# Tokenizer with one product for queries and keys in a new order; inverse deviations by logarithm and exponential

## Chip, cores and metric

The kernel runs on one core of a Trainium2 chip. The metric is the device time of one execution in microseconds (us), as the median of several runs. TensorE (PE) multiplies, with its weight loads (PEld) beside it; VectorE (DVE), ScalarE (ACT) and GpSimd (POOL) work on what it leaves in PSUM and in SBUF; SyncE (SP) issues most DMAs. Each engine takes its instructions strictly in the order in which they are written and is held up by semaphore waits only.

## What is computed

The input is 64 samples of 8192 values. A tokenizer makes 64 channels x 64 positions of each, and four residual layers follow, each on a layer-normed input:

```python
# tokenizer
h = maxpool(relu(bn(conv1d(h, w1, b1, 1, 1))), 8)
h = maxpool(relu(bn(conv1d(h, w2, b2, 1, 1))), 4)        # 64 channels x 128
q = Wq @ h + bq; k = Wk @ h + bk; v = Wv @ h + bv        # 8, 8 and 64 channels
h = gamma * (v @ softmax(q.T @ k).T) + h
h = bn(conv1d(h, w3, b3, 2, 1))                          # 64 x 64
# four layers
h = h + attention0(layernorm(h)) ; h = h + experts0(layernorm(h))     # attention0: norm, attention, norm, GELU MLP
h = h + attention1(layernorm(h)) ; h = h + experts1(layernorm(h))     # experts0 ends in a norm of its own
def _layernorm(x): return (x - m) / jnp.sqrt(v + 1e-5)
```

## The kernel before, in words

`PHASES` lists the stages: the tokenizer, a norm `n1` (in attention0 it is applied twice over, so it needs two inverse deviations, `twice=True`), attention0, `n2`, the GELU MLP, `n3`, experts0, `n5`, attention1, `n6`, experts1. Everything is FP32, and there is no planner: the order on each engine is the order in which the functions of a stage call each other.

**Tokenizer.** The 64 samples go through in eight groups of eight (`NG` = 8). For each group g: `conv1` (L251) makes four pieces h = 0 to 3, each into a pair of PSUM banks, and DVE's `reduce1` (L454) pools each piece; ACT's `relu1` (L557); `conv2` (L270) into banks 2 to 5, two `reduce2` (L470), ACT's `pooled` (L577); `keys_queries` (L296), one product for the keys into bank 2 and one for the queries into bank 3, which ACT copies out with its bias (L583, `t_k` and `t_q`); `values` (L306) and its copy (L589); `energy` (L315), DVE's `maxima` (L463), ACT's eight `exps` (L571), DVE's `soften` (L474 to L480), which normalises half of the probabilities while POOL's `half` (L226) does the other half; `turn` (L323) transposes them on PE and ACT's `turned` (L595) copies them out; `attend` (L332), DVE's `add` (L487) of the residual, `conv3` (L284), ACT's `last` (L561), which writes `h`, and DVE's `count` (L649), the statistics for the norm.

`steps` writes this as a `first()`, a `rest(g, b)` for g = 1, a loop of `rest` over g = 2 to 5, and four more calls of `rest` for g = 6 to 9 in which `among` leaves out what is not there. One `rest(g)` works on four groups at once: `turn(g-1)`, `keys_queries(g)`, `energy(g)`, `conv2(g+1)`, the pieces of `conv1` of groups g+1 and g+2, and `attend(g-2)` and `conv3(g-2)`. `weights(0..3)` (L346) are products of weights for attention1 that are done in gaps at the end, and `m.early[...]` are steps of attention0 that are called there.

**Loads.** SP issues the small constants and the first half of group 0, then (`load_rest`) all constants of the tokenizer in one DMA of 704 KB, group 1 of the input, then (`load_layers`) 3101, 1024 and 512 KB for the later stages, and only then, as PSUM and buffers allow, groups 2 to 7.

**Norms.** `norm` gives three parts: `variance` on DVE, `deviation` on ACT (`Sqrt` of variance + 1e-5, L690; for `n1` a second one, L692) and `inverse` on DVE (a `reciprocal`, L698; for `n1` also L701). Each norm is done for the first 48 samples and for the last 16 apart, and the calls stand inside the stages around it. experts0 has its own: `deviation` (L1801) and `normal` (L1671), once in each of its 16 groups of four samples, and in each group also one `Exp` for the gate (L1796). ACT needs a table for a function; where the next function is not in the one that is loaded, an `ACT_TABLE_LOAD` stands before it, written out (`preload_act_table`) or put in by the compiler.

## Time and profile before

| | us |
|---|---|
| median of 3 runs | 986.7 (983.88, 986.7, 989.49) |
| profiled execution | 982.16 |
| its span | 980.4 |
| tokenizer, to its last write of `h` | about 159 |
| experts0, the part in which all groups are alike | 340 to 570 |
| TensorE busy over the span | 924.4 (94%) |
| ScalarE busy over the span | 642.8 (66%) |

The profiled execution is one of its own, 4.5 us under the median of the three timed runs; the three lie 5.6 us apart. In the profile, a row of the timeline gives start, duration, engine, source line, operation, the tiles it writes and reads, their shapes and the number of merged instructions; the bracket at its end is the idle time of that engine just before, and what ended it. A table by stretches gives the busy time of each engine and the granted TensorE clock (1.0 is 2.4 GHz, 0.5 is 1.2 GHz, a value between is a mix of the two over the stretch).

### The profile page before, as it was taken

To read this page: it belongs to the slowest core of one execution; us is meant where nothing else is said; L and a number is where in the kernel's file an instruction comes from. 1 tells how busy PE (TensorE), PEld (TensorE's weight loads), DVE (VectorE), ACT (ScalarE), POOL (GpSimd) and SP (SyncE) were. 2 spreads that over 40 slices of the span, in tenths; PEclk is the share of its full clock that TensorE was granted. 3 is DMA by queue.
4 is the path that set the end of the run, shared out by engine and by line. 5 is a ranking of instruction groups with operands and counts; after the bars stand their busy time and mean duration, and the time that the engine had idled before them with its cause. 6 is when DMAs were issued, how large, how long until landed. Compare 5 with 4: busy or idle time off the path is not lost. (4 is left out here: it accounts for less than half of the span.)

```text
span 980.4 us, 35512 instructions
## 1 busy us (share of the span) xinstructions
PE 924.4 (94%) x12674; PEld 670.1 (68%) x12674; DVE 702.7 (72%) x1964; ACT 642.8 (66%) x1205; POOL 518.7 (53%) x814
## 2 busy tenths in 40 slices
PE   7899988999798999999999997899999999969998
PEld 2355556777566888888888884566666666658887
DVE  4577745777666577877878778788888888875553
ACT  1245556888666677877878775777777777754444
POOL 0001015888684578787887875455555656452110
PEclk8899998999999999999999998999999999999999
DMA  8624000000000000000000000000000000000001
GB/s 281 110 34 64 0 2 1 2 0 0 2 1 1 3 3 3 0 0 0 0 0 0 1 3 1 1 3 0 0 0 0 0 0 0 1 2 18 21 21 28
DMA packets 10961, 14.89 MB, mean 15 GB/s; under 512 B 9392, under 2 KB 9520, under 8 KB 9968
## 3 DMA queue, kind: packets, MB, share of 16 engines
q1 hardware_dynamic: 10704, 13.63, 6.1%
q8 instruction: 41, 0.67, 0.3%
q10 hardware_dynamic: 192, 0.39, 0.2%
q14 instruction: 24, 0.20, 0.1%
HBM read 11.92 MB, written 2.10 MB: 14 GB/s over the span
## 5 line engine op out<-in xcount | busy, mean ns | idle before, releaser
L1807 ACT ACTIVATE e_hid<-ps,cst 128x512 f32<-128x512 f32 x256 | 155.1, 687 | 53.7 <-PE ps L1579 53.7
L1514 POOL TENSOR_TENSOR e_acc<-e_acc,e_part 128x512 f32<-128x512 f32 x96 | 122.2, 1273 | 34.1 <-DVE e_part L1735 27.1
L1591 PEld LDWEIGHTS ps<-ew,e_hid 128*64 128x64 f32 x4096 | 124.8, 138 | 21.9 <-issue 10.4
L1591 PE MATMUL ps<-ew,e_hid 128*64 128x64 f32 x4096 | 133.8, 224 | 0.0
L1579 PE MATMUL ps<-e_xs,ew 64*128 64x256 f32 x1024 | 129.7, 393 | 0.0
L1735 DVE TENSOR_TENSOR e_part<-ps,e_wt 128x512 f32<-128x512 f32 x128 | 86.8, 687 | 44.5 <-PE ps L1591 39.6
L1579 PEld LDWEIGHTS ps<-e_xs,ew 64*128 64x128 f32 x1024 | 94.6, 189 | 15.7 <-issue 2.7
L2004 POOL TENSOR_TENSOR a_sum<-a_part 128x256 f32<-128x256 f32 x64 | 46.5, 727 | 94.0 <-DVE a_part L2112 93.9
L2073 PEld LDWEIGHTS ps<-cst,a_ex 128*128 128x128 f32 x512 | 56.6, 143 | 50.7 <-issue 50.7
L2101 DVE TENSOR_REDUCE a_rmax<-ps 128x8 f32<-128x1024 f32 x64 | 78.1, 1221 | 14.9 <-PE ps L2065 13.0
L226 POOL TENSOR_TENSOR t_prob<-t_ex,t_rscale 128x512 f32<-128x512 f32 x8 | 11.9, 1491 | 133.2 <-DVE t_rscale L477 133.2
L2104 DVE TENSOR_TENSOR a_diff<-ps,a_rmax 128x1024 f32<-128x1024 f32 x64 | 78.3, 1224 | 2.9
L2065 PE MATMUL ps<-a_u,a_xs 64*128 64x512 f32 x256 | 71.7, 637 | 8.3 <-DVE a_diff L2104 7.4
L2163 ACT ACTIVATE a_prob<-ps 128x1024 f32<-128x1024 f32 x64 | 65.5, 1023 | 17.7 <-PE ps L2073 17.2
L2089 PE MATMUL ps<-a_v,a_prob 128*64 128x66 f32 x2048 | 74.1, 224 | 0.6 <-DVE a_part L2112 0.6
L2073 PE MATMUL ps<-cst,a_ex 128*128 128x128 f32 x512 | 71.8, 283 | 1.6 <-ACT a_ex L2158 1.5
L2089 PEld LDWEIGHTS ps<-a_v,a_prob 128*64 128x64 f32 x2048 | 65.2, 137 | 11.4 <-issue 11.2
L2385 ACT ACTIVATE e_hid<-ps,cst 128x512 f32<-128x512 f32 x64 | 38.7, 687 | 50.4 <-PE ps L2261 50.4
L2158 ACT ACTIVATE a_ex<-a_diff 128x1024 f32<-128x1024 f32 x64 | 67.3, 1052 | 4.1 <-DVE a_diff L2104 3.5
L2146 ACT ACTIVATE a_u<-ps 128x1024 f32<-128x1024 f32 x32 | 32.8, 1025 | 34.6 <-PE ps L2041 34.6
L454 DVE TENSOR_REDUCE c_max<-ps 128x128 f32<-128x1024 f32 x32 | 38.9, 1222 | 15.7 <-PE ps L251 15.6
L2112 DVE TENSOR_TENSOR a_part<-ps,a_rec 128x512 f32<-128x512 f32 x64 | 44.3, 692 | 6.7
(258 smaller groups left out, 1994.0 us busy)
## 6 DMA issues: line engine op xcount, KB each, us to landing
x_in<-x_dram SPq DMA_DIRECT2D x42, 128.0 KB, 4.8
cst<-cst_dram SPq DMA_DIRECT2D x1, 3101.0 KB, 13.0
out_dram<-e_res SPq DMA_DIRECT2D x16, 128.0 KB, 2.0
ew<-ew_dram SPq DMA_DIRECT2D x1, 1024.0 KB, 15.1
cst<-cst_dram SPq DMA_DIRECT2D x1, 704.0 KB, 5.1
ew<-ew_dram SPq DMA_DIRECT2D x1, 512.0 KB, 16.9
x_in<-x_dram ACTq DMA_DIRECT2D x6, 64.0 KB, 3.7
x_in<-x_dram SPq DMA_DIRECT2D x6, 64.0 KB, 3.8
```

Source lines behind the costliest of these rows:

```text
L1514: eng.tensor_tensor(acc[:, :, :, :], acc[:, :, :, :], part[n % RING][:, :, :, :], ALU.add).then_inc(sum_sb.sem, 1)
L1579: mm = eng.matmul(m.ps[:, 4 - 2 * (n % 2) + r, j * 256:(j + 1) * 256], w1[rows, e * F0:(e + 1) * F0], T.xs[b][rows, :], start=True, stop=True)
L1591: mm = eng.matmul(m.ps[rows, 6 + n % 2, to:to + C], hid[e % 8][:, a:a + C], w2[:, e * C:e * C + C], start=True, stop=True)
L1735: eng.tensor_tensor(part[n % RING][:, :, :, :], m.ps[:, 6 + n % 2, :].rearrange("p (s j c) -> p s j c", s=TS, j=2), wt[b][:, :, 2 * n:2 * ...
L1807: nc.scalar.activation(hid[e % 8][:, :].rearrange("p (r t) -> p r t", r=2), m.ps[:, 4 - 2 * (n % 2):6 - 2 * (n % 2), j * 256:(j + 1) * 256 ...
L2065: mm = eng.matmul(m.ps[:, 2 + h, :], T.xs[b][rows, s * P:(s + 1) * P], u[b][rows, s, :, :].rearrange("p h t -> p (h t)"), start=True, stop ...
L2073: mm = eng.transpose(m.ps[:, 4 + j // 4, (j % 4) * P:(j % 4 + 1) * P], ex[s % 2][:, j, :], col(m, "ident"))
L2089: mm = eng.matmul(m.ps[rows, 6 + j // 4, (j % 4) * P:(j % 4) * P + W], prob[s % 2][:, j, rows], v[b][:, s, head * V:head * V + W], start=T ...
L2101: eng.tensor_reduce(rmax[:, :], src, AX, ALU.max).then_inc(max_sb.sem, 1)
L2104: eng.tensor_tensor(diff[:, :, :], src, bc(rmax[:, :], [P, H, P]), ALU.subtract).then_inc(diff_sb.sem, 1)
L2158: nc.scalar.activation(ex[s % 2][:, :, :], diff[:, :, :], ACT.Exp).then_inc(exp_sb.sem, 1)
L2163: nc.scalar.activation(prob[s % 2][:, :, :], m.ps[:, 4:6, :].rearrange("p a (j t) -> p (a j) t", t=P), ACT.Identity).then_inc(prob_sb.sem, 1)
```

## The change

It has four parts.

1. **One product.** The weights of keys and queries go into one matrix `wqk`, 64 columns for each of the two samples of a pair: columns 0 to 7 for the query and 32 to 39 for the key. `keys_queries` is one matmul into bank 2. ACT then makes two copies of 32 partitions for `k_sb` (which POOL has zeroed once, so that all other partitions are 0) and one of 128 partitions for `q_sb`: three activations in the place of two.
2. **A new order.** In a round, `attend` and `add` are of group g-1, not g-2, and stand just ahead of `energy(g)`; `values(g)` is in round g; `conv3(g-2)` follows the first `conv1` piece. On ACT `pooled` comes first and the exps are split 3 + 5, not 7 + 1. `first()` takes pieces 0 and 1 of group 1 ahead of `conv2(0)` (piece 1 into banks 6 and 7) with one matmul on zeros between them. The last rounds are written out as `tail()`, with `keys_queries(7)` and `values(7)` ahead of `turn(6)` and the four `weights` spread over it.
3. **Loads.** The weights of `conv2` have a DMA of their own ahead of group 1; the rest of the tokenizer's constants comes behind group 1.
4. **Inverse deviations.** `Sqrt` and `reciprocal` are replaced by `Ln` (of variance + eps), `Exp` with scale -0.5, and one Newton step on DVE of three small dependent instructions. `Ln` and `Exp` are in one table set (`LOGS`), which is loaded once at the start and again around the GELU MLP. `n1` has two of them and one more small DVE instruction.

The diff, cut to its core; the first `rest` is ScalarE's, the second VectorE's, and the last `deviation` is that of experts0.

```diff
-COLS += [("ident", P), ("w2", 3 * P), ("wq", P), ("wk", P), ("wv", P), ("w3", 4 * P)]
+COLS += [("w2", 3 * P)]
+TOK_B = sum(w for _, w in COLS)
+COLS += [("ident", P), ("wqk", P), ("wv", P), ("w3", 4 * P)]
...
-            for n, w in enumerate(("wk", "wq")):
-                eng.matmul(m.ps[:, 2 + n, :], col(m, w), x2[b][:, :], start=True, stop=True).then_inc(kq_ps.sem, 1)
+            eng.matmul(m.ps[:, kq_bank(g), :], col(m, "wqk"), x2[b][:, :], start=True, stop=True).then_inc(kq_ps.sem, 1)
...
         def rest(g, b):
+            pooled(g, b)
+            exps(g - 1, range(0, 3))
+            relu1(g + 1, 1 - b)
+            if known(g, 2):
+                last(g - 2)
+            exps(g - 1, range(3, GS))
+            turned(g - 1)
+            keys_queries(g)
+            values(g, b)
...
         def rest(g, b):
+            reduce1(g + 1, 1 - b, 3)
+            reduce1(g + 2, b, 0)
+            soften(g - 1)
+            reduce2(g + 1, 0)
+            reduce2(g + 1, 1)
+            reduce1(g + 2, b, 1)
+            if known(g, 2):
+                count(g - 2)
+            reduce1(g + 2, b, 2)
+            add(g - 1, 1 - b)
+            maxima(g)
...
         def keys_queries(g):
             eng.wait_ge(energy_ps.sem, energy_ps.at(g - 1))
+            eng.wait_ge(kq_ps.sem, kq_ps.at(g))
+            for rows in HALVES:
+                to, at = slice(rows.start, rows.start + 32), slice(rows.start + 32, rows.stop)
+                nc.scalar.activation(k_sb[to, :], m.ps[at, bank, :], ACT.Identity,
+                                     bias=col(m, "bk", at)).then_inc(kq_sb.sem, 1)
+            nc.scalar.activation(q_sb[:, :], m.ps[:, bank, :], ACT.Identity, bias=col(m, "bq")).then_inc(kq_sb.sem, 1)
...
-            nc.scalar.activation(dev[:, sl], var[:, sl], ACT.Sqrt, bias=m.eps[:, :]).then_inc(std_sb, 1)
+            nc.scalar.activation(log[:, sl], var[:, sl], ACT.Ln, bias=m.eps[:, :]).then_inc(log_sb, 1)
+            eng.wait_ge(log_sb, per * n + 1)
+            nc.scalar.activation(dev[:, sl], log[:, sl], ACT.Exp, scale=-0.5).then_inc(std_sb, 1)
...
+        def refine(eng, sl, first, v, shift, to, count):
+            eng.scalar_tensor_tensor(out=diff[:, sl], in0=first[:, sl], scalar=-0.5, in1=first[:, sl],
+                                     op0=ALU.mult, op1=ALU.mult).then_inc(root_sb, 1)
+            eng.wait_ge(root_sb, count + 1)
+            eng.scalar_tensor_tensor(out=m2[:, sl], in0=v[:, sl], scalar=shift, in1=diff[:, sl],
+                                     op0=ALU.add, op1=ALU.mult).then_inc(root_sb, 1)
+            eng.wait_ge(root_sb, count + 2)
+            eng.scalar_tensor_tensor(out=to[:, sl], in0=m2[:, sl], scalar=1.5, in1=first[:, sl],
+                                     op0=ALU.add, op1=ALU.mult).then_inc(ready, 1)
...
         def deviation(g):
-            nc.scalar.activation(y_dev[:, :], y_var[:, :], ACT.Sqrt, bias=m.eps[:, :]).then_inc(dev_sb.sem, 1)
+            nc.scalar.activation(y_log[:, :], y_var[:, :], ACT.Ln, bias=m.eps[:, :]).then_inc(log_sb.sem, 1)
+            eng.wait_ge(log_sb.sem, log_sb.at(g))
+            nc.scalar.activation(y_dev[:, :], y_log[:, :], ACT.Exp, scale=-0.5).then_inc(dev_sb.sem, 1)
```

**The start, on TensorE.** These are the first matmuls of before: four pieces of `conv1` of group 0 (L251, two matmuls each), `conv2(0)` (L270), three pieces of group 1, keys and queries (L296), the fourth piece, values (L306), piece 0 of group 2, energy (L315).

```order
L251 MATMUL ps<-x_in,w1s 128x512 x8
L270 MATMUL ps<-c,w2s 128x512 x12
L251 MATMUL ps<-x_in,w1s 128x512 x6
L296 MATMUL ps<-x,cst 128x512 x2
L251 MATMUL ps<-x_in,w1s 128x512 x2
L306 MATMUL ps<-cst,x 128x128 x4
L251 MATMUL ps<-x_in,w1s 128x512 x2
L315 MATMUL ps<-t_k,t_q 128x128 x8
```

And after, where the same steps are L268, L287, L312, L322 and L333, and L375 is the matmul on zeros:

```order
L268 MATMUL ps<-x_in,w1s 128x512 x10
L375 MATMUL ps<-warm 128x512
L268 MATMUL ps<-x_in,w1s 128x512 x2
L287 MATMUL ps<-c,w2s 128x512 x12
L268 MATMUL ps<-x_in,w1s 128x512 x4
L312 MATMUL ps<-x,cst 128x512
L322 MATMUL ps<-cst,x 128x128 x4
L268 MATMUL ps<-x_in,w1s 128x512 x2
L333 MATMUL ps<-t_k,t_q 128x128 x8
```

All of group 1's `conv1` now comes before keys and queries of group 0; piece 0 of group 2 still comes just ahead of the energy of group 0.

**A round of the loop, on TensorE,** from the transposes (before L323) to the energy. Before:

```order
L323 MATMUL ps<-cst,t_prob 128x128 x8
L246 ISA
L251 MATMUL ps<-x_in,w1s 128x512 x2
L292 ISA
L296 MATMUL ps<-x,cst 128x512 x2
L246 REGISTER_ALU
L251 MATMUL ps<-x_in,w1s 128x512 x2
L315 MATMUL ps<-t_k,t_q 128x128 x8
```

After (L341 transposes, L352 is `attend`):

```order
L341 MATMUL ps<-cst,t_prob 128x128 x8
L261 ISA
L268 MATMUL ps<-x_in,w1s 128x512 x2
L311 ISA
L312 MATMUL ps<-x,cst 128x512
L320 REGISTER_ALU
L322 MATMUL ps<-cst,x 128x128 x4
L261 REGISTER_ALU
L268 MATMUL ps<-x_in,w1s 128x512 x2
L352 MATMUL ps<-t_probT,v_tok 64x128 x8
L327 ISA
L333 MATMUL ps<-t_k,t_q 128x128 x8
```

Between the keys and queries and the energy that needs them stood one piece of `conv1`; now values, a piece of `conv1` and `attend` stand there. The first product's second matmul is gone.

**One group of experts0, on ScalarE,** from the gate's exponential to the norm's. Before:

```order
L1796 ACT_TABLE_LOAD
L1796 ACTIVATE e_gexp<-e_gap 128x4
L1805 REGISTER_ALU
L1807 ACTIVATE e_hid<-ps,cst 128x512 x2
L1805 REGISTER_ALU
L1807 ACTIVATE e_hid<-ps,cst 128x512 x2
L1799 ISA
L1800 REGISTER_ALU
L1801 ACT_TABLE_LOAD
L1801 ACTIVATE e_y_dev<-e_y_var,eps 128x4
```

After:

```order
L1860 ACTIVATE e_gexp<-e_gap 128x4
L1871 REGISTER_ALU
L1873 ACTIVATE e_hid<-ps,cst 128x512 x2
L1871 REGISTER_ALU
L1873 ACTIVATE e_hid<-ps,cst 128x512 x2
L1863 ISA
L1864 REGISTER_ALU
L1865 ACTIVATE e_y_log<-e_y_var,eps 128x4
L1867 ACTIVATE e_y_dev<-e_y_log 128x4
```

Both table loads of a group are gone, and one small activation is added. In the whole program 8 loads are left; they are at the start, around the GELU MLP and at the start of experts0.

## Rows read from the trace of the kernel before

**Rows 1.** Stretches of the span: length, busy time (instructions) per engine, clock.

```profile
0.00:31.25 31.25, 22.73 (x76) 8.86 (x76) 14.65 (x28) 7.32 (x11) 1.06 (x13) 0.89 0.91 266
61.42:124.33 62.91, 59.37 (x428) 33.09 (x429) 47.41 (x78) 31.55 (x95) 5.92 (x4) 1.00 0.22 32
124.33:158.20 33.87, 30.23 (x244) 22.17 (x244) 16.08 (x57) 18.66 (x53) 8.91 (x12) 0.95 0.01 1
340.00:570.00 230.00, 230.00 (x4401) 194.10 (x4403) 182.38 (x634) 175.38 (x295) 180.66 (x210) 1.00 0.00 1
```

**Rows 2.** Timeline of TensorE's matmuls in one round of the tokenizer's loop.

```profile
77.23 2.86 PE L270 MATMUL ps<-c,w2s 32*128 32x512 f32 x24 [0.33 <-ACT h L561]
...
81.65 1.13 PE L251 MATMUL ps<-x_in,w1s 48*128 48x512 f32 x4
82.71 1.98 PE L296 MATMUL ps<-x,cst 128*128 128x512 f32 x4
84.63 1.13 PE L251 MATMUL ps<-x_in,w1s 48*128 48x512 f32 x4
...
86.58 1.16 PE L306 MATMUL ps<-cst,x 128*128 128x128 f32 x8
87.67 1.09 PE L332 MATMUL ps<-t_probT,v_tok 128*64 128x128 f32 x16
...
93.00 2.86 PE L270 MATMUL ps<-c,w2s 32*128 32x512 f32 x24 [0.32 <-ACT h L561]
```

**Rows 3.** Timeline of the other engines in the same round.

```profile
84.73 0.69 ACT L583 ACTIVATE t_q<-ps,cst 128x512 f32<-128x512 f32 x1 [0.17 <-PE ps L296]
...
86.94 1.21 DVE L463 TENSOR_REDUCE t_nmax<-ps 128x8 f32<-128x1024 f32 x1
...
91.13 0.72 ACT L557 ACTIVATE c<-c_max,bi 128x512 f32<-128x512 f32 x1 [0.25 <-DVE c_max L454]
...
91.97 0.78 ACT L561 ACTIVATE h<-ps,bi,sc 128x512 f32 x1
```

**Rows 4.** Timeline of TensorE's matmuls in the first rounds.

```profile
14.28 5.50 PE L270 MATMUL ps<-c,w2s 32*128 32x512 f32 x24 [3.13 <-ACT c L557]
...
28.75 1.16 PE L306 MATMUL ps<-cst,x 128*128 128x128 f32 x8
31.26 1.13 PE L251 MATMUL ps<-x_in,w1s 48*128 48x512 f32 x4 [1.35 <-DMA x_in<-x_dram]
...
45.34 3.78 PE L270 MATMUL ps<-c,w2s 32*128 32x512 f32 x24
49.05 1.10 PE L323 MATMUL ps<-cst,t_prob 128*128 128x128 f32 x8
```

**Rows 5.** Timeline of the tokenizer's last rounds.

```profile
138.12 0.66 PE L323 MATMUL ps<-cst,t_prob 128*128 128x128 f32 x4 [1.47 <-DVE t_prob L480]
...
139.59 3.49 PE L296 MATMUL ps<-x,cst 128*128 128x512 f32 x4
...
158.32 0.78 ACT L561 ACTIVATE h<-ps,bi,sc 128x512 f32<-128x512 f32 x1 [1.24 <-PE ps L284]
```

**Rows 6.** Groups by line: table loads in experts0's loop (count, busy us, mean ns, idle before).

```profile
L1796 ACT ACT_TABLE_LOAD x13 | 16.7, 1283 | 0.2
L1801 ACT ACT_TABLE_LOAD x13 | 16.7, 1283 | 5.3 <-DVE e_y_var L1666 5.2
```

**Rows 7.** Timeline at four norms: n1, n3, n5 (late part), n6.

```profile
147.07 0.21 DVE L681 SCALAR_TENSOR_TENSOR norm_var<-norm_m,norm_dd 128x48 f32<-128x48 f32 x1
...
309.35 0.44 DVE L698 RECIPROCAL norm_rstd<-norm_dev 128x48 f32<-128x48 f32 x1
...
311.46 0.44 PE L793 MATMUL ps<-cst,e_xn 128*128 128x128 f32 x2 [3.14 <-POOL e_xn L781]
...
620.11 0.25 DVE L698 RECIPROCAL norm_rstd<-norm_dev 128x16 f32<-128x16 f32 x1 [2.69 <-ACT norm_dev L690]
...
865.61 1.07 PE L2073 MATMUL ps<-cst,a_ex 128*128 128x128 f32 x8 [1.26 <-ACT a_ex L2158]
```

More of the change, by code:

```diff
@@ L179, in steps, with known, pair, kq_bank @@
             rest(2 * i + 1, 1)
-        for g in range(NG - 2, NG + 2):
-            rest(g, g % 2)
-    def among(g, first=0, last=NG - 1):
-        return not isinstance(g, int) or first <= g <= last
+        tail()
+    def known(g, least):
+        return not isinstance(g, int) or g >= least
+    def pair(g, h):
+        return 0 if not isinstance(g, int) or g > 1 else 2 * h if g == 0 else 6 * (h % 2)
+    def kq_bank(g):
+        return 5 if isinstance(g, int) and g == NG - 1 else 2
     def load_half(eng, g, b, r, some=slice(0, H2), sem=None):
@@ L370, in rest @@
         def rest(g, b):
-            if among(g, 2, NG - 2):
-                values(g - 1, 1 - b)
-            last = not among(g, 0, NG)
-            tail = not among(g, 0, NG - 1) and not last
-            if last:
-                weights(3)
-            if among(g, 2, NG + 1):
-                attend(g - 2, b)
-            if among(g, 1, NG - 2):
-                conv1(g + 1, 1 - b, 3)
-            if tail:
-                weights(0)
-                m.early["a0_biases"](eng)
-            if last:
-                m.early["a0_turn"](eng)
@@ L411, in pe @@
         eng.wait_ge(prep, 1)
-        steps(eng, first, rest)
+        steps(eng, first, rest, tail)
     def dve(eng):
@@ L543, in dve @@
         m.left["tokenizer"] = last
-        steps(eng, first, rest)
+        steps(eng, first, rest, tail)
     def act(eng):
```

311 lines of the change are left out of this document (173 added, 138 removed).

## The prediction

> **What bounds the kernel now.** I read the table by stretches first [rows 1]: it tells which engine is full where. In the tokenizer's steady part, 61.42 to 124.33, TensorE is busy 59.37 of 62.91 us at full clock, DVE 47.41 and ACT 31.55; so TensorE is the bound there. In experts0, 340 to 570, TensorE is busy 230.00 of 230.00 us. At the two ends of the tokenizer it isn't full: up to 31.25 us it has 22.73 us of work at a mean clock of 0.89, in the last rounds 30.23 of 33.87 us at 0.95. The timelines of a round, of the start and of the end say what the gaps wait for [rows 2 to 5], and the groups by line what the table loads amount to [rows 6].
>
> **Part 1, one product less.** In a round the two products take from 82.71 to 84.63, 1.92 us [rows 2]; one takes half, 0.96. A round goes from the `conv2` at 77.23 to the one at 93.00, 15.77 us (62.91 over four rounds is 15.73), and holds about 0.3 us of waiting, for ACT's copy of `h`. If nothing else comes late, it becomes 14.8.
>
> **Part 2, is anything late in the new round?** I follow it from the start of `conv2` (time 0). Up to the next `conv1` piece, at 4.42 (81.65), nothing changes on PE: `conv2` and the transposes, which wait for soften. The five exps that now stand behind `h` on ACT take 5 x 0.34 = 1.7 us, soften some 0.6 to its scale, POOL's half 1.5: 3.85 with the 0.05 of starting late, where POOL ended at 3.8 before (81.01). So the transposes end where they did. Then: piece 4.42, product 5.48, values 6.44, piece 7.53, `attend` 8.55, energy 9.57, ending at 10.6. Energy needs three copies on ACT instead of two; each is 0.69 [rows 3], whatever its number of partitions I take it, since the row is for 512 elements a partition; 6.5 + 0.1 + 3 x 0.65 = 8.6, under 9.57: the third copy, 0.69 us, is hidden by values and `attend` (1.09 and 1.02, [rows 2]), with 1.0 to spare. Behind the energy PE has a piece, `conv3` and a piece: 1.02 + 1.93 + 1.03 = 4.0, to 14.6. On the other side DVE takes maxima 1.21 and a pooling of 1.23, then ACT `relu1` 0.72 and `h` 0.78 [rows 3]: 10.7 + 1.2 + 1.2 + 0.8 + 0.8 = 14.7, and `conv2` starts 0.25 later, at 14.95. The round is therefore 15.0, of which 0.35 is again a wait for `h`: **0.75 us less per round**, not the full 0.96. It holds for `conv2(2)` to `conv2(7)`, five rounds: 3.75 us. Bounds: 0 (something else is late by as much) and 5 x 0.96 = 4.8.
>
> **Part 3, the start.** The new order has group 1's `conv1` done early, since piece 0 needs no pooling of group 0 beyond the second. conv2(0) started at 14.28 after 3.13 us of idle and ran 5.50 us instead of 2.86, at the low level of the clock [rows 4]; now it starts at the same time (DVE's fold of the weights, `relu1`) but after pieces of group 1, so perhaps at full clock. Group 0's values then end near 22.6 instead of 29.9. It does not help: the next step, piece 0 of group 2, waits at 31.26 for its input [rows 4], and that DMA stands in SP's queue behind the same 4.6 MB for the later stages and only 64 KB less in front; I take the same 31.2. So TensorE stands idle for some 8.6 us, where it stood for 1.35. After 3.13 us of idle the clock was low for 5.5 us of work [rows 4]; I take it low until about 36. Then, with the durations of the low clock: piece to 33.2, energy 35.0, piece 36.6, conv2(1) 39.5 (37.6 before), two poolings and a third to 43.1, piece 3 of group 2 to 44.2, its pooling 45.5, conv2(2) 46.6 to 49.5 at the high clock, 51.8 at the low one. Before, it ended at 49.05 with 3.78 us for itself, partly low. I take **1.0 us later**; bounds: 2.7 later, and 0.6 earlier if the clock stays high throughout.
>
> The Trainium skill bears on this, on the page TensorE: Matmul & The Clock Gate (Part 1): a TensorE that has idled goes back to half clock, and is given full clock only after sustained work. By that rule the matmul on zeros protects conv2(0), where nothing is gained, and not the wait at 31 us. The trace agrees as far as it goes (5.50 us against 2.86 for the same `conv2`).
>
> **Part 4, the last rounds.** From conv2(7) at 124.33 to `h` of group 7 at 158.32 it is 34.0 us [rows 5]. There `turn(6)` waited 1.47 us for soften, and then the two products of group 7 ran at the low clock, 3.49 us. In `tail()` they are one product and stand ahead of `turn(6)`. Walking through as above from conv2(7) = 0: `turn(5)` to 4.5, a part of the weights 5.5, product 6.5, values, weights, `attend` 9.6, energy(6) 10.6; conv3(5) 12.6, product and values of group 7 to 14.7; DVE's maxima 11.9, ACT's eight exps 14.85, soften, POOL's half 17.0, `turn(6)` 17.7, `turned` 18.8, energy(7) 20.0, maxima 21.3, exps of group 7 to 24.4 (149.28 - 124.33 = 24.95 before). From there 0.85 us more goes, because before `turn(7)` stood behind eight weight products. Sum **1.4 us earlier**. Bounds: 0.5 later (the 1.5 us wait at 14.7 lowers the clock again) and 2.9 earlier (the 0.96 + 1.9 us that the second product cost in the two rounds, all of it on the path).
>
> **Part 5, the table loads.** Of 44 loads of 1283 ns, 36 go. 26 of them, 33.4 us of ACT time, are in experts0 [rows 6]. **They are hidden**: TensorE is busy for all 230 us of that stretch, and ACT for 175.38. Bounds: 0, and 33.4 if ACT were the bound. The new instructions there, one of ACT (0.3) and two of DVE (0.2 each) in a group of 17.25 us, are hidden in the same way: DVE has (230 - 182.38) = 47.6 us free, 3.6 in a group. What remains are the places where PE stands. Late part of n5: DVE waits 2.69 us for the deviation, whose load is in front of it [rows 7]; without the load it comes 0.93 earlier, the Newton step takes three times 0.25 (one such is 0.21, [rows 7]) where the reciprocal took 0.25: 0.3 gained. n6: PE waits 1.26 us for an exp that comes behind a load [rows 7]; DVE, with the longer Newton step in front of its next pooling, gives only 0.4. n2, n2's late part and n3 keep their loads of the GELU and get 0.3 to 0.4 us longer each, on the way to POOL, for whose result PE stands 3.14 us at n3 [rows 7]: 1.1 lost. n1 is even (ACT 0.8 earlier, DVE 1.3 later). n6's late part 0.1 lost. Together **0.5 us lost**; bounds 2.5 lost, 2 gained.
>
> The skill's page ScalarE: Activation LUTs (Rules for kernel authors) says to budget some 2.7 us for each switch of the table set; the rows have 1283 ns. By 2.7 us the two places that gain would gain about 2.8 us more in all, and the time would be 980.
>
> **The sum.** -3.75 + 1.0 - 1.4 + 0.5 = -3.65 us. The profiled execution of 982.16 becomes 978.5. It lies 4.5 us under the median of the three runs, 986.7; I keep that distance and forecast **983.0** for the median. What a measurement of this kernel can tell from no change is about 0.5%, 4.9 us, and the three runs of before are 5.6 us apart. So a gain of 3.65 us reads as the same.
>
> **Rivals.**
> A. *The start isn't lost.* If the clock recovers at once after the wait for group 2 and stays high in the last rounds, the start gives 0.6, the end 2.9: 3.75 + 0.6 + 2.9 - 0.5 = 6.75 us, 979.9. For it: in before, after 1.35 us of idle there, the clock stayed high. Against it: the idle is six times as long now.
> B. *The new round chains through `add` and `pooled`: slower.* On ACT `pooled(g+1)` now stands ahead of the exps of group g, and it waits for `add(g-1)`, which waits for `attend`, at 9.6: 10.7 to 11.4 in my count, and the exps can start at 12.0. The slack is 0.65 us. From the point where `add` is later than that, each round passes from PE to DVE, ACT and back, `relu1` and `h` behind the exps, and PE stands. At 1.0 us more than before per round it is +5.0, with +1.0 -1.4 + 0.5: 5.1 us slower, 991.8. Against it: DVE's pooling before `add` ends at 9.9, and POOL is out of it.
> C. *The loads did cost.* The weight loads of PE wait here and there for `e_hid`; if a third of the 33.4 us were on the path, 11 more us go, 972. Against it the 230.00 of 230.00.
> D. *No gain.* The start loses its 2.7, the end nothing gained and 0.5 lost on norms: 0.55 us earlier, 986.2.
>
> **Chances.** Forecast 0.49, A 0.28, D 0.11, B 0.08, C 0.04. Faster by over 0.5%: A, C, and 0.06 of the forecast's own spread, 0.38. Slower: B, 0.08. Within: 0.54. The range goes from A less the 2.8 us that half the spread of the three runs makes, 977, to D plus as much, 989; it leaves out C and B.
>
> **What would show it.** The steady round: `conv2` to `conv2` near 15.0 us. One product of 1.0 us. Piece 0 of group 2 again near 31.2 with an idle of 8 to 9 us before it, and 2 us long. conv2(2) ending at 49.5 to 52. `h` of group 7 near 32.6 us behind conv2(7). experts0's group again 17.25 us, with ACT some 30 us less busy. I am wrong if group 2 lands well before 31 us, if the round is over 15.5, or if experts0 gets shorter.

## The result and the profile after

| | before | after |
|---|---|---|
| median of 7 runs each, us | 985.3 (983.5 to 989.5) | 989.7 (988.2 to 993.0) |
| ratio, 95% interval | | 1.0042 [1.0024, 1.0061] |
| profiled execution, us | 982.16 | 988.21 |
| span, us; mean granted clock | 980.4; 0.977 | 986.5; 0.965 |
| busy PE, DVE, ACT, us | 924.4, 702.7, 642.8 | 928.5, 741.0, 606.7 |

The changed kernel is 4 us slower, and the interval excludes a ratio of 1; 983.0 with 977 to 989 was forecast. The first view is again the table by stretches: length, busy time of PE, PEld, DVE, ACT and POOL, granted clock, DMA. Its four rows answer to [rows 1].

```profile
0.00:31.98 31.98, 24.88 (x76) 9.45 (x76) 14.53 (x28) 7.18 (x12) 1.53 (x14) 0.84 0.95 258
63.55:121.90 58.35, 55.53 (x428) 32.54 (x429) 44.41 (x76) 34.14 (x99) 5.93 (x4) 1.00 0.23 34
121.90:157.16 35.26, 30.75 (x233) 23.92 (x234) 18.65 (x62) 19.77 (x64) 8.31 (x12) 0.85 0.01 1
340.00:570.00 230.00, 229.60 (x4392) 193.22 (x4390) 211.20 (x644) 143.24 (x280) 179.90 (x210) 1.00 0.00 1
```

The steady part is 58.35 us where it was 62.91. The last rounds, from `conv2(7)` to `h` of group 7, are 35.26 us where they were 34.0, and at a mean clock of 0.85 where it was 0.95. In experts0 no table load of [rows 6] is left and ACT is 32 us less busy, as forecast; DVE is 29 us busier, which was not.

The timeline of TensorE in a round, which answers to [rows 2]:

```profile
78.30 2.86 PE L287 MATMUL ps<-c,w2s 32*128 32x512 f32 x24 [0.65 <-ACT h L587]
...
83.46 1.12 PE L312 MATMUL ps<-x,cst 128*128 128x512 f32 x2
84.42 1.05 PE L322 MATMUL ps<-cst,x 128*128 128x128 f32 x8
...
87.49 1.16 PE L333 MATMUL ps<-t_k,t_q 64*128 64x128 f32 x16
...
92.72 0.71 PE L287 MATMUL ps<-c,w2s 32*128 32x512 f32 x4 [0.49 <-ACT h L587]
```

One product of 0.96 us (83.46 to 84.42) and a round of 14.42; over four rounds 58.35 / 4 = 14.59, against 15.73. The third copy is hidden, the energy waits for nothing, and 0.5 us of waiting for `h` is left.

The first rounds, which answer to [rows 4]:

```profile
14.13 2.08 PE L268 MATMUL ps<-x_in,w1s 48*128 48x512 f32 x4 [2.60 <-DMA x_in<-x_dram]
...
20.15 4.81 PE L287 MATMUL ps<-c,w2s 32*128 32x512 f32 x24
...
31.98 1.13 PE L268 MATMUL ps<-x_in,w1s 48*128 48x512 f32 x4 [1.70 <-DMA x_in<-x_dram]
...
41.96 2.08 PE L268 MATMUL ps<-x_in,w1s 48*128 48x512 f32 x4 [2.55 <-DVE c_max L478]
...
47.47 4.81 PE L287 MATMUL ps<-c,w2s 32*128 32x512 f32 x24
52.21 1.09 PE L341 MATMUL ps<-cst,t_prob 128*128 128x128 f32 x8
```

TensorE now waits for group 1's input too (until 14.13), and `conv2(0)` runs at 20.15, where it ran at 14.28. `turn(0)` is at 52.21, 3.2 us later than in [rows 4]. The wait of 2.55 us at 41.96 is one of the new order. It was 1.42 at the same place before (the first two lines are DVE's in after, the third is TensorE's in before):

```profile
38.42 2.36 DVE L494 TENSOR_REDUCE c_max<-ps 128x256 f32<-128x1024 f32 x2 [1.58 <-PE ps L287]
40.69 1.21 DVE L478 TENSOR_REDUCE c_max<-ps 128x128 f32<-128x1024 f32 x1
40.11 1.81 PE L251 MATMUL ps<-x_in,w1s 48*128 48x512 f32 x4 [1.42 <-DVE c_max L454]
```

DVE now does both `reduce2` of `conv2(1)` ahead of the `reduce1` for which the next piece of `conv1` waits. Before, it did one. The two pieces behind this wait take 2.08 us each and `conv2(2)` takes 4.81; at the high level they take 1.13 and 2.86. The last rounds, which answer to [rows 5]:

```profile
138.85 1.10 PE L341 MATMUL ps<-cst,t_prob 128*128 128x128 f32 x8 [2.69 <-DVE t_prob L504]
...
141.39 2.02 PE L333 MATMUL ps<-t_k,t_q 64*128 64x128 f32 x15
143.33 1.97 PE L352 MATMUL ps<-t_probT,v_tok 128*64 128x128 f32 x16
...
147.63 3.30 PE L301 MATMUL ps<-x,cst 64*128 64x256 f32 x15
```

`turn(6)` waits 2.69 us (1.47 in [rows 5]), and behind it TensorE runs at its low level: an `energy` of 16 products that takes 1.16 in the steady round takes 2.02 for 15. The groups by line of DVE in experts0's loop (345 to 545) have what is new there:

```profile
L1734 DVE SCALAR_TENSOR_TENSOR e_y_rstd<-e_y_root,e_y_dev 128x4 f32<-128x4 f32 x11 | 8.3, 758 | 0.4
L1781 DVE TENSOR_SCALAR e_den<-e_gexp 128x4 f32<-128x4 f32 x12 | 7.2, 599 | 0.0
L1728 DVE SCALAR_TENSOR_TENSOR e_y_root<-e_y_dev 128x4 f32<-128x4 f32 x11 | 7.1, 641 | 0.0
L1731 DVE SCALAR_TENSOR_TENSOR e_y_root<-e_y_var,e_y_root 128x4 f32<-128x4 f32 x11 | 6.7, 611 | 0.4
```

The three instructions of the Newton step take 0.61 to 0.76 us each, on four elements a partition; I had counted 0.2.

**One execution is not the kernel.** Over 17 to 35 executions in each later comparison, before had medians of 986.3 to 987.5 and a mean granted clock of 0.972; the profiled one, with 0.977 and 982.16, was quicker than any of these. So part of what two single traces show as lost between them is the clock of that one execution. Where I can, I therefore compare groups of traces: six have the old tokenizer with its loads (before, norms_only, old_logexp and the three probes), five have the new one as it was written (after, tok_only, x0_logexp, x0_sqrt, logexp_all).

| us, mean (range) | six old | five new | difference |
|---|---|---|---|
| `turn(0)` starts | 49.8 (47.6 to 51.3) | 53.6 (52.2 to 54.3) | +3.8 |
| `turn(0)` to `conv2(7)` | 75.3 in each | 69.7 in each | -5.6 |
| `conv2(7)` to `h` of group 7 | 32.9 (32.3 to 34.0) | 35.8 (35.3 to 36.1) | +2.9 |
| `h` of group 7 starts | 158.0 (156.9 to 158.9) | 159.0 (157.2 to 160.0) | +1.1 |

### The profile page after: what moved, and what is told of

It is laid out like the page before. It is cut to its first block and busy times, and to the rows that moved or that the text cites. A ratio compares the mean times of both kernels' runs of the same rounds, so it can differ in the third digit from the quotient of the medians.

```text
span 986.5 us, 35690 instructions
## 1 busy us (share of the span) xinstructions
PE 928.5 (94%) x12660; PEld 674.0 (68%) x12660; DVE 741.0 (75%) x2022; ACT 606.7 (61%) x1205; POOL 518.5 (53%) x815
## 5 line engine op out<-in xcount | busy, mean ns | idle before, releaser
L1571 POOL TENSOR_TENSOR e_acc<-e_acc,e_part 128x512 f32<-128x512 f32 x96 | 122.4, 1275 | 31.2 <-DVE e_part L1799 24.1
```

The source lines that it names most:

```text
L1571: eng.tensor_tensor(acc[:, :, :, :], acc[:, :, :, :], part[n % RING][:, :, :, :], ALU.add).then_inc(sum_sb.sem, 1)
```

## The experiments

All medians are in us. The medians of before moved by 1 to 2 us between comparisons, so ratios are compared; 0.001 is 1 us. Where two kernels are compared through their ratios to before and the intervals overlap, the text says so.

| kernel | median | before beside it | ratio, 95% interval |
|---|---|---|---|
| tok_only | 988.3 | 986.3 | 1.0016 [1.0002, 1.0030] |
| norms_only | 991.0 | 986.3 | 1.0057 [1.0043, 1.0072] |
| x0_sqrt | 995.4 | 986.3 | 1.0085 [1.0072, 1.0099] |
| x0_logexp | 988.5 | 986.3 | 1.0026 [1.0010, 1.0042] |
| start_inputs | 985.9 | 986.5 | 0.9990 [0.9976, 1.0005] |
| tail_weights | 989.9 | 986.5 | 1.0023 [1.0005, 1.0042] |
| probe_two_inputs | 986.6 | 986.5 | 0.9993 [0.9976, 1.0009] |
| probe_one_input | 986.0 | 986.5 | 0.9998 [0.9980, 1.0015] |
| probe_chain | 987.6 | 986.4 | 1.0012 [0.9996, 1.0028] |
| tail_busy | 987.8 | 987.5 | 1.0006 [0.9987, 1.0024] |
| logexp_all | 984.7 | 987.3 | 0.9974 [0.9956, 0.9992] |
| old_logexp | 983.8 | 987.3 | 0.9958 [0.9944, 0.9973] |
| old_start_logexp | 982.3 | 987.3 | 0.9934 [0.9906, 0.9962] |
| old_start_hold | 979.8 | 986.4 | 0.9934 [0.9914, 0.9954] |
| start_old_norms | 981.3 | 987.5 | 0.9940 [0.9919, 0.9961] |
| start_logexp | 977.8 | 987.5 | 0.9893 [0.9861, 0.9925] |
| start_busy_logexp | 974.6 | 987.5 | 0.9864 [0.9843, 0.9886] |
| hold_more | 971.1 | 987.3 | 0.9840 [0.9813, 0.9867] |

### Which half costs: tok_only and norms_only

The tokenizer's part of the change (with its loads) alone, and the deviations' part alone.

> The kernel before with the tokenizer of after alone (one product, the new order, the new loads and the tail); all deviations are again square root and reciprocal, with their table loads. In the trace of after the tokenizer ends 1.2 us earlier than in before, and what is lost comes behind it: 0.4 at the start of attention0, 2.1 at n2 and the MLP's entry, 1.5 at n3, 2.8 in experts0, 1.6 at n6, against 1.3 gained at n5. Theory N (the norms cost it): the time is 1 to 3 us under before, 983 to 984.5, and the low-clock stretch at n2 is 3.4 us long again. Rival S (the losses behind the tokenizer come from where its new end lets the clock fall, not from the norms): at least the 2.1 at n2 comes back, and the time is 986 to 990. My forecast's own sum without its part on norms would be 4.1 under before, 981.2.

> The kernel before with the new deviations alone (logarithm, exponential and a Newton step in all norms and in experts0), old tokenizer. Theory N: about 6 to 7 us over before, 991 to 992; experts0's DVE is some 9.6 us busier in four groups (69 us) and PE waits for e_part in the last groups. Rival S: about 1 to 3 us over before, with the 2.8 of experts0 alone. My forecast's term for the norms was 0.5 us over before.

Measured: +1.6 us and +5.6 us. Neither half gains. Theory N expected a gain of 1 to 3 us of the tokenizer; that fell, and the time is in S's 986 to 990. For the norms N came near (6 to 7 expected, S had 1 to 3), and my forecast's +0.5 fell. The two halves don't add up to after's 4.2; why they don't was not tried. tok_only has a mean granted clock of 0.963 over its 12 executions where before has 0.972: its rounds are as short as after's, and it gives the time back at the start and at its end. In the five new traces `conv2(7)` is at 121.9 to 124.0, against 122.9 to 126.6 in the six old ones; and the last `conv3` is at 155.0 to 156.8, against 154.8 to 156.8. The lead of 1.8 us on the mean at `conv2(7)` is gone at the end of the tail.

### The start: start_inputs

```diff
         m.load_rest(eng)
+        eng.wait_ge(conv1_ps.sem, conv1_ps.at(0))
+        for r in range(2):
+            load_half(eng, 2, 0, r)
         m.load_layers(eng)
+        eng.wait_ge(conv1_ps.sem, conv1_ps.at(1))
+        for r in range(2):
+            load_half(eng, 3, 1, r)
-        with eng.Fori(1, NG // 2) as i:
+        with eng.Fori(2, NG // 2) as i:
```

> After with one change on SP: the input of group 2 is asked for as soon as group 0's conv1 has run, ahead of the 4.6 MB for the later stages, and group 3's right behind them. In the traces with the new tokenizer PE stands 1.7 to 5.4 us before the first conv1 piece of group 2 (at 32 to 33 us), with the input as the releaser. Theory Q (the start is lost to that transfer's place in the queue): the wait for the input goes, group 2's piece starts by 30, conv2(2) starts 2 to 4 us earlier than the 47.5 to 49.8 of the new kernels, and the time is 986 to 988 where after has 989.7. Rival P (the start is lost to PE's order: the pooling chain between conv2(1), the third and fourth piece and conv2(2) is what is late): conv2(2) stays within 1 us, and so does the time.

Theory Q held. TensorE's timeline of this kernel:

```profile
28.67 1.13 PE L274 MATMUL ps<-x_in,w1s 48*128 48x512 f32 x4
...
38.66 1.93 PE L274 MATMUL ps<-x_in,w1s 48*128 48x512 f32 x4 [2.55 <-DVE c_max L484]
...
47.60 1.09 PE L347 MATMUL ps<-cst,t_prob 128*128 128x128 f32 x8
```

The first piece of group 2 is at 28.67 and waits for nothing, and `turn(0)` is at 47.60, 4.6 us earlier than in after. By the ratios it is 5 us less than after, and the intervals don't overlap. So the place of the transfer in the queue is worth 5 us to the new order, which needs its inputs earlier than the old one did and was left with them behind 4.6 MB. The wait of 2.55 us for the pooling is as in after: P's chain is real too, is not touched by this run, and is 1.1 us of what the new start is behind the old one.

### The tail: tail_weights and tail_busy

tail_weights moves `weights(2)` and `weights(3)` to between `values(7)` and `turn(6)`.

> After with one change on PE: the third and fourth part of the weight products stand between values(7) and turn(6), where the third stood before attend(5) and the fourth behind turn(6). In all traces of the new tokenizer turn(6) waits 2.69 us for soften, and a low clock stretch of 7 to 10 us follows; in before the wait is 1.47. Theory W (the tail lost its 2 us to that wait and to the clock behind it): 2 us of work fill it, attend(5) and energy(6) come 1 us earlier, and from conv2(7) to the last conv3 it is 31 to 32 us instead of 32.3 to 33.4; the time is 1 to 2 us less than after's. Rival V (the chain exps, soften, turn is fixed by ACT and DVE and the clock falls anyway): nothing changes, 989.7.

The wait of `turn(6)` went from 2.69 to 0.80 us, but a new one of 1.20 for `t_probT` stood behind it. From `conv2(7)` to the last `conv3` it was 31.8 us, as theory W had it (31 to 32). The time is 2 us under after's by the ratios, but the intervals overlap, so that a gain in time is not shown. tail_busy adds work instead:

```diff
+        def zeros(n):
+            for _ in range(n):
+                eng.matmul(m.ps[:, 1, 3 * P:4 * P], m.warm[:, 0:P], m.warm[:, 0:P], start=True, stop=True)
             values(NG - 1, 1)
+            zeros(10)
             turn(NG - 2)
...
             conv3(NG - 2)
+            zeros(3)
             turn(NG - 1)
+            zeros(4)
             attend(NG - 1, 1)
```

> After, with products of 128 columns on zeros where TensorE stands in the last rounds: ten ahead of turn(6) (wait of 2.69 us), three ahead of turn(7), four ahead of attend(7) (1.11 us). No result is touched and no order changed. Theory K (the tail's gain is given back by the granted clock: at 130 to 180 us the profiles of the old tokenizer lose 3.4 to 5.1 us to the low level, those of the new one 6.8 to 10.2): the low stretches between 139 and 160 go or get shorter, from conv2(7) to the last conv3 it is 30.5 to 31.5 us instead of 32.3 to 33.4, and the time is 986 to 988. Rival V (the chains of exps, soften and turn set the tail's length, the low clock only fills waits): the stretch is as long as before and the time 989.7.

Its TensorE in the last rounds:

```profile
137.22 2.40 PE L407 MATMUL ps<-warm 128*128 128x128 f32 x20
140.09 1.10 PE L341 MATMUL ps<-cst,t_prob 128*128 128x128 f32 x8 [0.47 <-DVE t_prob L511]
...
142.39 1.16 PE L333 MATMUL ps<-t_k,t_q 64*128 64x128 f32 x16 [0.17 <-ACT t_probT L631]
143.48 1.09 PE L352 MATMUL ps<-t_probT,v_tok 128*64 128x128 f32 x16
...
145.81 2.00 PE L301 MATMUL ps<-x,cst 64*128 64x256 f32 x15
```

The same energy, attend and conv3 as in after (2.02, 1.97, 3.30) take 1.16, 1.09 and 2.00: TensorE stays at its high level. From `conv2(7)` (123.11) to the last `conv3` (153.84) it is 30.7 us, where the five new traces have 32.3 to 33.4 and the six old ones 30.2 to 31.9. Theory K held: what the tail lost against the old one, it lost to the clock. But even so it is not shorter than the old one (30.7 on the mean too), so the forecast's gain there does not exist at the high level either. By the ratios tail_busy is 3.6 us under after, with intervals that just touch; start_busy_logexp below is 2.9 under its pair, with intervals that overlap.

### experts0: x0_logexp, x0_sqrt and three probes

x0_logexp (the diff) leaves out experts0's Newton step; x0_sqrt goes back to square root and reciprocal there and keeps the rest of after.

```diff
-            nc.scalar.activation(y_dev[:, :], y_log[:, :], ACT.Exp, scale=-0.5).then_inc(dev_sb.sem, 1)
+            nc.scalar.activation(y_dev[:, :], y_log[:, :], ACT.Exp, scale=0.5).then_inc(dev_sb.sem, 1)
-            eng.scalar_tensor_tensor(out=y_root[:, :], in0=y_dev[:, :], scalar=-0.5, in1=y_dev[:, :],
...
+            eng.reciprocal(y_rstd[:, :], y_dev[:, :]).then_inc(rstd_sb.sem, 1)
```

> After with experts0's Newton step left out: ACT takes the logarithm and the exponential of half of it, DVE one reciprocal as in before; the refinement of the root there isn't computed. No table loads in the loop and no two-input instructions of DVE in normal. Theory D: 986.8, as with the square root, since the loads are hidden; DVE's reciprocal 0.18 us. Rival H: 989.7, as after. If logarithm and exponential themselves cost (ACT's longer chain to the deviation), this kernel is slower than the one with the square root by what they cost.

> After with one part undone: the deviation of y in experts0 is again a square root on ACT and a reciprocal on DVE, with two table loads of 1.28 us in a group. Theory D (the three two-input DVE instructions of the Newton step wait for POOL's instructions and cost experts0 2.8 us): 986.8, experts0's group 17.25 us throughout, DVE some 2 us less busy in a group, ACT some 2.7 us busier. Rival H (DVE's extra time is hidden as I forecast, and the 2.8 us have another source): no difference from after, 989.7, and the drift stays. Rival C (the loads did cost): slower than after.

x0_logexp is 1.6 us under after by the ratios. Theory D said 2.8, and the intervals overlap, so the time alone shows nothing; the traces do. From the first to the fifteenth product with `e_wT` (one in a group), before has 236.92 us, x0_logexp 236.92 and after 238.00; norms_only, the other kernel with the step, 237.80. From there to the sixteenth it is 17.00 in before, 18.11 and 18.76. In logexp_all, which has no step in n5 either, it is 17.00 again. So about 1 us is lost in the loop (1.08 and 0.88) and 1.8 at its end, 0.65 of the latter by the step in experts0 and 1.1 by the one of n5.

x0_sqrt was expected at 986.8 and took 995.4, 4.3 us over after by the ratios. Its loop is 236.92 us: two loads of 1.28 us a group are hidden, as forecast. But n5 is done there too, and ACT, now with `Sqrt` around it, loads twice for its `Ln` and its `Exp`:

```profile
573.34 1.28 ACT L722 ACT_TABLE_LOAD   x1
574.64 0.34 ACT L722 ACTIVATE norm_log<-norm_var,eps 128x48 f32<-128x48 f32 x1
574.99 1.28 ACT L727 ACT_TABLE_LOAD   x1
576.28 0.24 ACT L727 ACTIVATE norm_dev<-norm_log 128x48 f32<-128x48 f32 x1
...
577.74 0.66 PE L1635 MATMUL ps<-e_xs,ew 64*128 64x256 f32 x2 [1.79 <-ACT e_hid L1863]
```

Two loads, 1.28 us each with the logarithm between them, keep ACT from `e_hid`, and TensorE waits 1.79 us: from the fifteenth to the sixteenth product with `e_wT` it is 20.62 us, 1.9 more than in after. Where the other 2.4 us are was not traced. A load was free where ACT had room before TensorE needed it, and here it hadn't. This mix of both ways is dearer than either way alone.

Why do the Newton instructions take 0.6 to 0.76 us? DVE and POOL of after, side by side in one group:

```profile
492.71 4.10 POOL L1571 TENSOR_TENSOR e_acc<-e_acc,e_part 128x512 f32<-128x512 f32 x3
...
494.38 1.02 DVE L1728 SCALAR_TENSOR_TENSOR e_y_root<-e_y_dev 128x4 f32<-128x4 f32 x1
495.44 0.16 DVE L1731 SCALAR_TENSOR_TENSOR e_y_root<-e_y_var,e_y_root 128x4 f32<-128x4 f32 x1
495.64 1.19 DVE L1734 SCALAR_TENSOR_TENSOR e_y_rstd<-e_y_root,e_y_dev 128x4 f32<-128x4 f32 x1
```

POOL's three `e_acc` follow each other from 492.71 to 496.81, some 1.37 us each, so they change at about 494.1 and 495.4. The first Newton instruction ends at 495.40, the third at 496.83, with POOL's; the second slips in at the change and takes 0.16. It is so in the whole stage. From 300 to 620 us after has 48 of these instructions. 25 take over 0.25 us, and each of them ends 15 to 22 ns after the POOL instruction that was running when it started; 20 of the 23 short ones start while POOL runs nothing. No semaphore stands between the two engines there: the opening says that an engine is held up by semaphore waits only, and these rows show that this is not all. The Trainium skill, page SBUF — State Buffer, section Who interferes with whom, says that a DVE instruction with two SBUF inputs contends with a GpSimd instruction that reads SBUF, and that the port pair which the two engines share is an exclusive lock. The rows agree (1.02 and 1.19 us against 0.16). Three probes in the kernel before, each with three more instructions whose results nobody reads:

> The kernel before with three more instructions of DVE behind the reciprocal of experts0's deviation: the same two-input form as the first of the Newton step, [128x4] from a tile of its own memory to another that nobody reads. Theory D (such an instruction starts only when POOL's running instruction ends): they take 0.6 to 0.7 us each on the mean instead of 0.16 to 0.2, ending where POOL's e_acc instructions end; DVE is about 2 us busier in a group, and experts0 is 1 to 2 us longer. Rival H: 0.17 each and no time.

> The kernel before with three more reciprocals [128x4] at the same place, into tiles that nobody reads. Theory D: they don't wait for POOL, 0.16 to 0.18 us each, DVE 0.5 us busier in a group, no time. If they take 0.6 too, then it isn't the form of the instruction but its place behind e_part or the statistics that costs.

> The kernel before with three dependent two-input instructions of DVE behind the reciprocal in experts0, the Newton step's own three with its waits, into tiles that nobody reads. Theory E (between two dependent instructions there is a gap of some 0.04 us in which POOL's next instruction starts, and the second waits for its end): 0.6 to 0.7 us each, DVE some 25 us busier in 200 us of experts0's loop, the loop 1 us longer over its 14 groups, as in after; the time 1 to 3 us over before. Rival (it was the place, or the exponential coming later): 0.3 us each as with the independent three, and no time.

The groups by line of probe_one_input, probe_two_inputs and probe_chain over 345 to 545:

```profile
L1674 DVE RECIPROCAL e_y_probe<-e_y_dev 128x4 f32<-128x4 f32 x33 | 3.0, 151 | 0.0
```

```profile
L1674 DVE SCALAR_TENSOR_TENSOR e_y_probe<-e_y_dev 128x4 f32<-128x4 f32 x33 | 8.9, 322 | 0.0
```

```profile
L1680 DVE SCALAR_TENSOR_TENSOR e_y_probe<-e_y_probe,e_y_dev 128x4 f32<-128x4 f32 x11 | 13.1, 1189 | 0.4
L1674 DVE SCALAR_TENSOR_TENSOR e_y_probe<-e_y_dev 128x4 f32<-128x4 f32 x11 | 7.4, 674 | 0.0
L1677 DVE SCALAR_TENSOR_TENSOR e_y_probe<-e_y_var,e_y_probe 128x4 f32<-128x4 f32 x11 | 1.8, 162 | 0.4
```

One input: 0.15 each, no wait for POOL, although 45 of the 48 in the stage start while a POOL instruction runs. Two inputs, independent: 0.32 on the mean; in the timeline the first waits for POOL and the other two run right behind it. Two inputs, dependent: 0.68 on the mean, (7.4 + 1.8 + 13.1) / 33, since in the gap of 0.04 us between two of them POOL starts its next instruction. So form and dependence together make it dear, as theory E says. None of the probes cost a time that can be told from none, and all three left the loop at 236.9 us; there E was wrong, which expected 1 us, and so was D, which expected 0.6 to 0.7 each for the independent ones. The table by stretches has it for before, probe_chain and after:

```profile
345.00:545.00 200.00, 200.00 (x3852) 168.85 (x3850) 157.44 (x538) 154.45 (x259) 159.57 (x188) 1.00 0.00 1
```

```profile
345.00:545.00 200.00, 200.00 (x3851) 168.98 (x3849) 174.51 (x581) 153.29 (x256) 158.95 (x186) 1.00 0.00 1
```

```profile
345.00:545.00 200.00, 199.66 (x3859) 168.53 (x3856) 184.25 (x558) 125.68 (x247) 156.88 (x184) 1.00 0.00 1
```

DVE is busy for 157.4, 174.5 and 184.3 us of the 200, and only in the last is TensorE not full. At the loop's end, at 578.12 and 580.48, it waits 0.28 and 1.20 us there for `e_part`. Whether it is DVE's fill as such or the later `e_yn`, which in the probe does not hang on the chain, is not separated.

### The other norms, and whether the new tokenizer is worth it: logexp_all, old_logexp, old_start_logexp

The Newton step is left out in every norm (`Exp` with 0.5, one reciprocal), in after and in norms_only; old_start_logexp has start_inputs' transfers too.

> After without the Newton step in any norm (exponential of half the logarithm, one reciprocal), nothing else changed. Experts0 alone gave 1.2 us. Theory M (the chain of three to six dependent DVE instructions costs at every wait of a norm): 3 to 5 us under after, 985 to 986.5. Rival (the 6 us of the combined kernel came from the order of the transfers): 988, as with experts0 alone.

> The old tokenizer with the same deviations without Newton steps. Norms with Newton steps took 5 us more than before; the steps are worth 3 to 5 us, and the loads that go at n5 some 1: 985 to 987, about before. If the new tokenizer as it stands gains nothing over the old one, this is within 1 us of the run with the new tokenizer and the same norms.

> The same with groups 2 and 3 asked for ahead of the 4.6 MB. The old start waits 0.5 to 1.4 us for group 2's input at 31 to 33 us where the new one waits up to 5.4, so the gain is 1 to 2 us at most: 984 to 986. The new tokenizer with it and the same norms took 977.8; a difference of 5 us and more is what the new rounds give (5 times 1.14 = 5.7).

From 1.0042 to 0.9974 is 6.8 us for all Newton steps in after, and from 1.0057 to 0.9958 9.9 us in norms_only: more than theory M's 3 to 5, and in neither pair do the intervals overlap. Of the 6.8 the stretch of experts0 above holds 2.8; the rest was not traced place by place. One place, n6, in after and then in logexp_all:

```profile
868.35 0.20 DVE L734 SCALAR_TENSOR_TENSOR norm_diff<-norm_dev 128x48 f32<-128x48 f32 x1
868.58 0.72 DVE L737 SCALAR_TENSOR_TENSOR norm_m<-norm_var,norm_diff 128x48 f32<-128x48 f32 x1
869.34 0.49 DVE L740 SCALAR_TENSOR_TENSOR norm_rstd<-norm_m,norm_dev 128x48 f32<-128x48 f32 x1
...
872.29 1.13 PE L2131 MATMUL ps<-a_u,a_xs 64*128 64x512 f32 x4 [1.43 <-DVE a_diff L2170]
```

```profile
861.09 0.44 DVE L746 RECIPROCAL norm_rstd<-norm_dev 128x48 f32<-128x48 f32 x1
...
863.97 1.13 PE L2118 MATMUL ps<-a_u,a_xs 64*128 64x512 f32 x4 [0.38 <-DVE a_diff L2157]
```

TensorE waits 1.43 us instead of 0.38, for a DVE that was 1.48 us with the step instead of 0.44. And the logarithm itself pays: logexp_all is 4.2 us under tok_only, which differs from it by the square roots and their loads alone. old_logexp is as much under before, and start_logexp below is 4.7 under start_old_norms (intervals that overlap by a little). What these kernels leave out is the refinement of the root.

The two tokenizers with the same cheap deviations: 0.9974 new, 0.9958 old. As it was written, the new one gains nothing. With the earlier transfers it is 0.9893 (start_logexp, which also has group 1's input moved) against 0.9934, some 4 us better where 5 and more were expected; the intervals overlap a little, so the size is not settled. In the old order the transfers gave 2.4 us by the ratios, with overlapping intervals too.

### Together: start_logexp, start_old_norms, start_busy_logexp, hold_more, old_start_hold

start_logexp is logexp_all with start_inputs' transfers and group 1's input ahead of the weights of `conv2`; start_old_norms the same with square roots; start_busy_logexp adds tail_busy's products; hold_more adds seven products on zeros of 128 columns in attention0's first round, behind `turn(1)`, where in start_busy_logexp TensorE waits 1.88 us for `a_xs`. old_start_hold is old_start_logexp with these seven.

> After with the earlier transfers of groups 2 and 3, the input of group 1 ahead of the weights of conv2, and without the Newton step in any norm (exponential of half the logarithm, one reciprocal; the refinement isn't computed). From the runs so far: 3.7 for the transfers, 1.2 for experts0's Newton step, and for the other norms' steps at the waits of n1, n2, n3, n5, n6 some 1 to 3 more; so 981 to 984 where after has 989.7 and before 985.3 to 986.5. If the other norms' Newton steps cost nothing, 985.

> The new tokenizer with square roots and reciprocals in all norms, the earlier transfers of groups 2 and 3 and group 1's input ahead of the weights of conv2. The new tokenizer with the old norms took 988.3, 1.4 less than after; with the transfers' 3.7 it is 984 to 985. Against the kernel without Newton steps it says which way to a deviation is the cheaper one outside experts0: if they are within 1 us, the table loads were worth nothing at all, in the waits of n1 to n6 either.

> The same kernel with the products on zeros of the last rounds. Theory K: 2 to 3 us less than without them, 979 to 982. Rival V: no difference.

> The fastest kernel so far (earlier transfers, no Newton steps, products on zeros in the tail, 974.6) with seven more products of 128 columns on zeros in attention0's first round, where TensorE waits 1.88 us for a_xs and the clock is low for 7 to 10 us behind it. Theory K: the low stretch there goes or gets shorter, 1 to 3 us less, 972 to 973.5. Rival: the clock falls there for the wait behind it (0.4 to 2.5 us for a_q0T) and the time is 974.6.

> The old tokenizer with the early transfers, no Newton steps, and the seven products on zeros in attention0's first round. Where the clock is what costs there, 1 to 3 us less than the 982.3 without the products: 979.5 to 981. The new tokenizer with everything took 971.1, of which 3 came from the products in its own tail.

All four with the new tokenizer came out below what was expected. start_old_norms was to be within 1 us of start_logexp if the table loads were worth nothing; it is 4.7 above it. By the ratios the transfers (5.2 us) and the Newton steps (6.8) add up to 0.9922 for start_logexp. It has 0.9893, and 0.9922 is inside its interval, so a further gain of group 1's earlier place is not shown. Its trace has none at the first piece of group 1 either: it starts at 14.09 after a wait of 2.70 us for its input, and in after, with 192 KB more ahead of that input, at 14.13. The stretch 130 to 180 of start_logexp, start_busy_logexp and hold_more, the same view as at the top:

```profile
130.00:180.00 50.00, 41.23 (x298) 31.63 (x295) 25.92 (x98) 30.64 (x112) 22.33 (x40) 0.80 0.01 1
```

```profile
130.00:180.00 50.00, 44.71 (x378) 35.21 (x376) 29.91 (x112) 34.29 (x126) 27.37 (x49) 0.90 0.01 1
```

```profile
130.00:180.00 50.00, 44.77 (x419) 35.53 (x420) 33.12 (x123) 36.33 (x134) 31.02 (x55) 1.00 0.01 2
```

The clock goes from 0.80 to 0.90 to 1.00, and the median from 977.8 to 974.6 to 971.1. The intervals of neighbours overlap, so the size of one step is uncertain; the traces carry the cause. From the last `conv3` to the first `a_aT` product it is 19.66 us in start_busy_logexp (147.69 to 167.35) and 16.63 in hold_more (146.60 to 163.23). In old_start_hold the same stretch goes from 0.90 to 1.00 as well, but its ratio stays at 0.9934 with an interval of 0.4%: not decided there. hold_more is 1.6% under before, and 2% under after.

## Why the prediction was wrong, point by point

1. **The rounds** (part 2): right, in the mechanism and nearly in the size. Forecast 15.0 a round, where four rounds of the loop have 14.59 on the mean, 1.14 less than before. For five rounds -3.75 us was forecast; from `turn(0)` to `conv2(7)` it is -5.6. That is beyond the bound of 4.8, five times the product that went, so part of it is something else, which was not traced. The count behind the energy (14.7 for `h`) was 0.3 long.
2. **The start** (part 3): this step failed. Forecast +1.0 with a bound of +2.7; measured +3.2 at `turn(0)` in the two profiled executions and +3.8 between the groups. Up to `conv2(1)` the count was 1.1 too late (36.6, measured 35.50). From the start of `conv2(1)` to that of `conv2(2)` it has 10.0 us, and 12.0 were measured (11.6 to 12.0 in all five). The low clock was priced behind the wait for group 2 only, until 36. The wait for the poolings behind `conv2(1)`, 2.55 us instead of 1.42, is in the count, but nothing for what it does to the clock: the pieces behind it are counted at 1.1 us and took 2.08. `conv2(2)`, counted at 2.9 to 5.2, took 4.81. "Now it starts at the same time", of `conv2(0)`, was wrong too, since I took group 1's input as landed and it came at 14.13. This costs little by itself, since TensorE waits for group 2 either way: in tok_only `conv2(0)` is at 19.15, and TensorE stands 5.38 us before group 2's first piece at 32.70. That wait was placed well (31.98 against 31.2). start_inputs shows that the new order gains 5 us where it goes.
3. **The last rounds** (part 4): this step failed too. Forecast -1.4, bound +0.5; measured +1.3 from `conv2(7)` to `h` of group 7 (35.26 against 34.0) and +2.9 between the groups. `turn(6)` was at 16.95 us behind `conv2(7)`, earlier than the 17.7 that I counted. My own count leaves TensorE idle from 14.7 to 17.7, 3.0 us, and yet the bound speaks of a wait of 1.5 that "lowers the clock again", for 0.5 us. tail_busy shows 2.4 us for it in the trace (33.1 against 30.7), and no gain of the order without it.
4. **The norms** (part 5): the table loads in experts0 were hidden, as said; x0_sqrt's loop shows it, and rival C is out. The failed term is the new instructions, "0.2 each, hidden": 0.6 to 0.76 us each, because each is a two-input instruction that hangs on the one before and waits for POOL. Forecast +0.5 with a bound of 2.5; measured +2.6 on the new tokenizer (1.0016 to 1.0042, with intervals that overlap) and +5.6 on the old. All loads that go are worth 4.2 us (tok_only to logexp_all), the Newton steps cost 6.8.
5. **The anchor** (982.16 against the median): half sound. The gap between the profiled execution of before and its median was the clock of that execution, and stayed; but a sum that starts from that trace takes its high clock as a property of the kernel.
6. **The rivals.** D, no gain, with a start that loses its 2.7, was the nearest; no rival had the norms as a cost of several us, because I bounded the new instructions by a row of another place, 0.21 us at n1, where POOL was still.
7. **The signs.** None of the three signs of being wrong came: group 2 did not land early, the round was not over 15.5, experts0 did not get shorter. All three watched the steps that held. Among the other signs three failed: `h` of group 7 at 35.26 behind `conv2(7)` instead of 32.6, `conv2(2)` ending at 52.3 instead of 49.5 to 52, and 1.70 us of waiting before group 2's first piece instead of 8 to 9.

By the ratios: the tokenizer +1.6 and the norms +2.6 give the 4.2 us; the second of these is the rest that is left, not a measurement of its own. In the traces the tokenizer's part is +3.8 at the start, -5.6 in the rounds and +2.9 at the end.

## What to carry to other kernels

Price a small instruction by the place where it will stand, and look at what POOL runs there if it is one of DVE with two inputs; a chain of dependent ones can pay that price each time. When a new order makes a stage want its inputs earlier, move the transfers with it. And where TensorE must stand, the low clock behind the wait may be dearer than the wait: a few products on zeros held the clock, while moving work into the gap opened another one.
